# A two-layer decoder: filler products in waits of TensorE, and part of the next step's vector work between the two pieces of a double step

## The reference

```python
# layer 0
x = x + attention(ln(x))      # 1 head of 128, causal, softmax over the whole 512x512 matrix
x = x + cross(ln(x), ctx)     # 1 head, weights rounded to 256 levels, softmax over 77
x = x + experts(ln(x))        # 8 experts; each takes its own 128 tokens (top_k over tokens), GELU
# layer 1
x = x + attention(ln(x))      # 16 heads of 64, causal, softmax by row, output projection
x = x + cross_top(ln(x), ctx) # 16 heads of 8, the 32 largest of 77 scores per row, softmax, output projection
x = x + experts2(ln(x))       # 8 experts, each token takes its 2 best; relu(g) * u, then down
```

## Time and profile before

| | |
|---|---|
| median of 3 runs | 635.98 us (630.27 to 638.04) |
| the profiled execution | 634.84 us, span 633.10 us |
| PE busy | 545.8 us (86%) |
| PEld busy | 425.1 us (67%) |
| DVE busy | 409.1 us (65%) |
| ACT busy | 291.4 us (46%) |
| POOL busy | 208.6 us (33%) |
| mean granted clock | 0.937 |
| chain that ended last | PE 55%, DVE 20%, ACT 12%, issue 8%, POOL 5% |
| mean DMA rate | 30 GB/s |

### The profile page before, as it was taken

The page is one execution under the profiler, slowest core; times in us unless marked ns, Lnnn a source line. Parts: engine busy times, 40 slices in busy tenths (PEclk is TensorE's granted clock), DMA queues, the critical chain, the costliest instruction groups (busy, mean ns, idle before and its releaser), DMA issues.

```text
span 633.1 us, 11811 instructions
## 1 busy us (share of the span) xinstructions
PE 545.8 (86%) x3821; PEld 425.1 (67%) x3821; DVE 409.1 (65%) x2225; ACT 291.4 (46%) x721; POOL 208.6 (33%) x207
## 2 busy tenths in 40 slices
PE   4879768996789889899988688978977999899997
PEld 2565337874566656677667466658765878799997
DVE  3665654533443588886596698795895888844633
ACT  2332222333766565664764335562675555322221
POOL 4017200000434345653553335453363333250000
PEclk9996996997999999999999769896998999899999
DMA  4500101324000000000000000000440000010000
GB/s 136 166 1 15 50 13 51 104 63 150 2 1 1 1 1 3 0 2 2 1 2 1 2 0 2 2 2 1 158 139 0 19 14 19 18 35 1 26 1 9
DMA packets 23049, 19.16 MB, mean 30 GB/s; under 512 B 2048, under 2 KB 18508, under 8 KB 22989
## 3 DMA queue, kind: packets, MB, share of 16 engines
q1 hardware_dynamic: 22477, 17.36, 9.0%
q0 software_dynamic: 512, 1.05, 0.5%
HBM read 15.38 MB, written 3.01 MB: 29 GB/s over the span
## 4 chain that ended last, share of the span: by engine, by line
PE 55%; DVE 20%; ACT 12%; issue 8%; POOL 5%; DMA 0%; DVEq 0%; ACTq 0%; POOLq 0%
PE ps L1744 48%; DVE wk L1132 4%; ACT w_mem L1514 4%; DVE nmax L1068 3%; DVE top L1122 3%; ACT pr L1514 2%; ACT cat_mem L1498 2%; DVE sel_mem L961 2%; PE ps L2117 2%; PE ps L2179 1%; POOL xs_dram L737 1%; DVE xn L1095 1%; POOL wk L686 1%; POOL ex_mem L693 1%; PE ps L1756 1%
## 5 line engine op out<-in xcount | busy, mean ns | idle before, releaser
L1068 DVE TENSOR_REDUCE nmax<-ps 128x2 f32<-128x256 f32 (+1 forms) x64 | 51.2, 820 | 55.6 <-PE ps L1744 55.3
L1132 DVE MATCH_REPLACE8 wk<-top,wk 128x77 f32<-128x77 f32 x384 | 80.5, 223 | 0.0
L657 POOL TENSOR_TENSOR w_mem<-w_mem,rinv 128x256 f32<-128x256 f32 (+3 forms) x44 | 53.1, 1219 | 72.1 <-DVE rinv L1074 71.7
L1253 DVE TENSOR_TENSOR sel_mem<-gr,ps 128x512 f32<-128x512 f32 x47 | 32.2, 686 | 49.0 <-ACT gr L1687 48.2
L1744 PE MATMUL ps<-cat_mem 64*128 64x512 f32 (+7 forms) x272 | 54.4, 479 | 9.9 <-ACT cat_mem L1498 9.9
L1122 DVE MAX8 top<-wk 128x8 f32<-128x77 f32 x384 | 57.9, 223 | 0.0
L1687 ACT ACTIVATE gr<-ps 128x512 f32<-128x512 f32 x47 | 28.1, 598 | 63.1 <-PE ps L1744 63.1
L1514 ACT ACTIVATE w_mem<-ps,nmax 128x128 f32<-128x128 f32 (+3 forms) x88 | 44.5, 519 | 14.3 <-DVE nmax L1068 14.2
L595 POOL TENSOR_TENSOR rstd<-var_eps,minus_half 128x4 f32<-128x4 f32 x8 | 8.2, 1026 | 119.3 <-DVE var_eps L798 119.2
L686 POOL TENSOR_SCALAR wk<-wk 128x616 f32<-128x616 f32 x16 | 28.1, 1754 | 55.3 <-DVEq L1136 55.0
L657 POOL TENSOR_TENSOR pr<-pr,rinv 128x768 f32<-128x768 f32 (+3 forms) x20 | 26.7, 1343 | 34.9 <-DVE rinv L1074 34.8
(11 more groups left out here) (334 smaller groups left out, 1340.5 us busy)
## 6 DMA issues: line engine op xcount, KB each, us to landing
w_mem<-in_L_ffn_W_dram SPq DMA_DIRECT2D x12, 256.0 KB, 3.1
f_mem<-in_L_ffn_Wg_dram SPq DMA_DIRECT2D x8, 256.0 KB, 2.9
f_mem<-in_L_ffn_Wu_dram SPq DMA_DIRECT2D x8, 256.0 KB, 3.4
f_mem<-in_L_ffn_Wd_dram SPq DMA_DIRECT2D x8, 256.0 KB, 3.9
sel_mem<-in_L_ffn_W_dram SPq DMA_DIRECT2D x4, 256.0 KB, 4.9
xs_dram<-zero SPq DMA_DIRECT2D x1, 960.0 KB, 6.2
ys_dram<-f_mem SPq DMA_DIRECT2D x15, 64.0 KB, 1.5
xs<-xs_dram SPq DMA_DIRECT2D x3, 256.0 KB, 3.5
```

What stands on the lines that cost most here:

```text
L657: pool.tensor_tensor(pr[s][:, :, at:at + n], pr[s][:, :, at:at + n], rinv[:, i % 8, :].unsqueeze(2).to_broadcast([P, 2, n]), ALU.mult)\
L1068: dve.tensor_reduce(nmax[:, i % 8, :], ps[:, 2 * s:2 * s + 2, at:at + (c + 1) * P], X, ALU.max, negate=True).then_inc(nmax_ready, 1)
L1132: dve.match_replace(wk[q][:, t, h, :], top[q][:, t, h, 8 * r:8 * r + 8], src[:, t, h, :], GONE).then_inc(top_step, 1)
L1253: dve.tensor_tensor(hg[s][:, :], gr[s][:, :], ps[:, 2 * s + 1, :], ALU.mult)\
```

## The change

Five places get another order or one more instruction, and nine calls of `keep_busy` are added, which issue 65 filler products in all. Every output stays what it was.

- VectorE: `select(1, 1)` directly behind `select(0, 0)`.
- VectorE: `first_of(U)` holds what a step did first (`evac_cat`, `row_max(U+2)`, `row_inv(U+1)`); behind a double step U, `first_of(U+1)` is issued between pieces 2 and 3 of U.
- VectorE: `gate(13)` moves ahead of tile 12's piece.
- ScalarE: one GELU of a 128x1 column behind the exponential of the routing.
- TensorE: fillers in the last expert (6), before the rows of expert 0 are turned (4), before and behind the last scatter (4 and 4), before `norm_T(6)` (14), in `context_T` of steps 36 and 44 (4 each), in blocks 2 to 7 of the weight loading (3 each) and before `up_rows(0)` (7).

```diff
+def double_step(U):
+    n, r = piece_of(U) if 0 <= U < NU else (0, None)
+    return r == 2 and n >= 4
@@ VectorE, experts of layer 0
             select(0, 0)
+            select(1, 1)
             gate_of(0, 0)
             turn_sel(0, 0)
-            select(1, 1)
@@ VectorE, attention steps
-            for U in range(NU):
-                n, r = piece_of(U)
+            def first_of(U):
                 for j in range(4 * NP - 1):
                     if U == FIRST[j + 1] + 1:
                         evac_cat(j)
...
                     row_max(U + 2)
                 if U + 1 < NU:
                     row_inv(U + 1)
+            for U in range(NU):
+                n, r = piece_of(U)
+                if not double_step(U - 1):
+                    first_of(U)
...
                 if r is not None:
                     eight(n, r)
                     remove(n, r)
-                if r == 2 and n >= 4:
+                if double_step(U):
+                    first_of(U + 1)
                     eight(n, 3)
                     remove(n, 3)
@@ VectorE, experts of layer 1
             for j in range(NS):
-                gate(j)
+                if j != 13:
+                    gate(j)
...
                 if j == 12:
                     shares_of(1, 4, 2)
+                    gate(13)
                 cross(E + j)
@@ ScalarE
             act.activation(lg[:, :, :], lg[:, :, :], ACT.Exp)\
                .then_inc(elg_ready, 1)
+            act.activation(share0[:, 1:2], minus_half[:, 0:1], ACT.Gelu_apprx_tanh)
@@ TensorE, expert0
                 if e + 1 < E:
                     gather(e + 1, 1 - q)
                     spread(e + 1)
+                else:
+                    keep_busy(0, 6)
                 pe.wait_ge(h_ready, FC * (e + 1))
@@ TensorE, around the experts of layer 0
+            keep_busy(4, 4)
             turn_rows(0, 0)
...
                 expert0(e, e % 2)
+            keep_busy(0, 4)
             scatter(E - 1, 1)
+            keep_busy(0, 4)
@@ TensorE, context_T
+                if k < 2:
+                    keep_busy(7, 4)
                 pe.wait_ge(cn_ready, 2 * (k + 1))
@@ TensorE, start of layer 1
             pe.wait_ge(xin_ready, E)
+            keep_busy(4, 14)
             norm_T(6)
@@ TensorE, weight loading
+                if b >= 2:
+                    keep_busy(7, 3)
                 for k in range(2):
                     minus_hi(b, k)
...
             pe.wait_ge(w_lo_ready, 2 * E)
+            keep_busy(0, 7)
             up_rows(0)
```

More of the change, by code:

```diff
@@ L1160, in add_context @@
                 stats_two(k, gn_var)
-            row_max(0)
-            row_max(1)
-            row_inv(0)
-            for U in range(NU):
-                n, r = piece_of(U)
+            def first_of(U):
                 for j in range(4 * NP - 1):
@@ L1173, in _ @@
                     row_inv(U + 1)
+            row_max(0)
+            row_max(1)
+            row_inv(0)
+            for U in range(NU):
+                n, r = piece_of(U)
+                if not double_step(U - 1):
+                    first_of(U)
                 for k in range(3):
```

## The result

The changed kernel takes 644.56 us (median of 4 runs, 639.46 to 645.34) against 636.22 us (630.27 to 638.04) beside it: ratio 1.0113, 95% interval 1.0061 to 1.0165. The forecast was 626 us. The mean granted clock rose, from 0.937 to 0.950, and the kernel got slower all the same.

A forecast was written before the change was run, and what follows sets the result against it. TensorE was taken as the bound, over half the span, with twelve spells at 1.2 GHz. Terms -5.9 + 0.2 - 2.0 + 1.2 - 0.4 - 2.0 = -8.9 took 634.84 to 625.9, predicted 626 us; range 615 to 635.

The forecast's parts named there:

- The last expert, the scatter and the start of layer 1: Fillers there: +0.2 us for last expert, scatter and projections, -2.0 before norm_T(6) if the clock holds.
- the sum of the double steps: New order in steps 31, 34, 37, 40, 43, 46, with context_T fillers: +1.2 us, bounds -8 and +13.
- Step 31: Double step: fourth piece 1.3 us later, and TensorE waited for exactly the pick behind it: +1.3 us.
- Step 34: Double step: copy TensorE idled 3.52 us for comes 3.2 earlier, the pick is late next: -3.6 us.
- Steps 37 and 40: Double steps: TensorE's scores end after the third piece, VectorE stands before the fourth, partly taken up later: +2.0 us.
- Step 43: Double step: scores wait for a ScalarE copy, fourth piece slips 3.4 us, its turn had 0.21 spare: +3.4 us.
- Step 46: Double step: copy waits for half-clock products, slip paid back with more if the clock holds: -1.9 us.
- VectorE waits inside each pair: Rival, double steps: VectorE waits at the row maximum before the fourth piece: +13 instead of +1.2, 638 us; chance 0.10.
- The first rival: Double steps: the swap frees more, -6.8 us instead of +1.2, giving 618 us; chance 0.22.
- the third: Rival, all filler places: the clock does not hold and fillers cost time, together +7.5, or 642 us; chance 0.10.
- The port rival: GpSimd's mask holds VectorE's multiplications and last context's normalisation 2.6 us each: +5, 631 us; chance 0.06.
- gate(13): Layer 1's experts: gate moved ahead of the piece ends TensorE's 2.78 us wait, gate(14) late next: -2.0 us.

The follow-up runs named there:

- 3: The kernel before with the layer-0 edits alone: 628.57 us, ratio 0.9876.
- 5: Kernel 3 with the new order in all six double steps and ScalarE's copy of the cross scores no longer waiting for the fourth piece: 649.66 us, ratio 1.022.
- 9: Kernel 3 with the new order in steps 37 and 43 alone: 632.81 us, ratio 0.9966.
- 10: Kernel 3 with the new order in step 31 alone: 631.73 us, ratio 0.9956.
- 14: Kernel 3 with the new order in step 40 alone: 628.70 us, ratio 0.9870.
- 15: Kernel 3 with gate(13) ahead of tile 12's piece: 629.03 us, ratio 0.9795.
- 17: Kernel 12, but in step 34 only the copy between the pieces, row maximum and reciprocals back behind the fourth piece: 623.17 us, ratio 0.9796.
- 13: Kernel 3 with the new order in all six double steps and nothing else: 639.55 us, ratio 1.0106.
- 2: The kernel before with the new order of the double steps as its only edit: 653.04 us, ratio 1.017.
- 7: Kernel 3 with the new order in step 34 alone: 622.55 us, ratio 0.9665.
- 1: The changed kernel with the new order of the double steps undone, all else kept: 630.25 us, ratio 0.9874.
- 4: The changed kernel with the new order undone and gate(13) at its old place, layer 1's fillers kept: 629.14 us, ratio 0.9878.
- 12: Kernel 7 with step 37's addition of the context's projection put between the two pieces: 618.94 us, ratio 0.9741.
- 16: Kernel 12 with gate(13) forward and eight fillers in the wait for gate(14): 620.29 us, ratio 0.9810.

## Why the prediction was wrong

**What held.** The first experts: forecast -5.9, measured -6.1 (shift from +0.5 to -5.6), with the pitch and the whole clock that were named. The last expert, the scatter and the start of layer 1: forecast +0.2 - 2.0 = -1.8, measured -2.1. But that part does not hold in every execution: in seven of the seventeen traced kernels with these fillers (3, 5, 9, 10, 14, 15, 17) a spell of low clock that begins between 144 and 151 us takes 1.6 to 2.2 us of it back. The early GELU is within that. Weight loading: forecast -0.4; the shift goes from +7.97 to +7.82, -0.15. Kernel 3 shows layer 0's part by itself, -7.4 us in the median. (The 65 fillers come from eight added calls of `keep_busy`, not nine.)

**The step that failed** is the sum of the double steps, +1.2 in the forecast and +15.5 measured (+14.6 and +15.0 in kernels 13 and 2); the forecast's upper bound, +13, was too low. It failed in sign for step 46 and in size for steps 31, 37, 40 and 43:

- Step 31: forecast +1.3, the lengths of the moved instructions; measured +4.9. VectorE also waited for them (2.0 us), and the clock fell behind TensorE's two waits.
- Step 34: forecast -3.6, measured -4.7 in the changed kernel and -6.5 alone. The wait and the sign were right; the size beyond it is the clock's.
- Steps 37 and 40: forecast +2.0 together; measured +4.1 for 40 alone, and 37 is +3.0 in the changed kernel. I had counted the maxima's waits, not TensorE's wait for the addition behind the fourth piece, which grew from 0.5 us (layer 0's part) to 4.62 (kernel 9); with step 34 moved it was 2.47 already (kernel 7).
- Step 43: forecast +3.4; the fourth piece slipped by 3.2, and with what TensorE then waited for, 4.7 (37 and 43 alone: 7.3).
- Step 46: forecast -1.9, "paid back if the clock holds". Measured +4.3. The copy waited 3.85 us (437.94), and TensorE 3.56 us for the normalisation behind the fourth piece. The clock did not hold, and of the 4.3 us 3.4 are idle time.

Under all of them one thing was missing. I had followed from the fourth piece to the pick alone. Behind the same piece stand ScalarE's copy of the scores, the addition and the normalisation, each with TensorE waiting. The forecast put these waits at nothing. The runs show 12.7 us more idle time of TensorE in the stretch (kernel 13 against 3). The clock is not what was missing. Each of TensorE's waits of 2.4 to 4.6 us shown above in this stage does have a spell at 1.2 GHz behind or around it (from 325, 369, 396.5 and 441 us), but the kernel before has such spells too, and the mean clock of the stretch is 0.89 before and 0.90 after.

**The rivals.** "VectorE waits inside each pair" is what happened, with its place and the sign right. I gave it 0.10 and priced it at +13 for the stage. That the price comes so near is partly luck: it took +3.4 at each of five steps, while the fourth piece was to be held over 3 us in every pair; VectorE waited that long in step 46 alone. The argument against it, that the pieces and not TensorE are late, holds at step 34 alone. The first rival, that the swap frees more, is refuted by the sum. So is the third, that the clock does not hold, for the fillers of layer 0 (1.00 from 86 to 157 us). The port rival is refuted too: a normalisation beside the mask alone ran in 0.94 us, and beside a division with two inputs, and the pick behind it, in 3.43. VectorE first, then GpSimd:

```profile
376.19 3.43 DVE L1101 TENSOR_SCALAR xn<-x,mean_var,rstd 128x128 f32<-128x128 f32 x2
...
441.39 0.94 DVE L1101 TENSOR_SCALAR xn<-x,mean_var,rstd 128x128 f32<-128x128 f32 x2 [0.24 <-DVE wk L1138]
...
376.20 1.89 POOL L663 TENSOR_TENSOR w_mem<-w_mem,rinv 128x1024 f32<-128x1024 f32 x1
...
441.30 1.75 POOL L692 TENSOR_SCALAR wk<-wk 128x616 f32<-128x616 f32 x1 [7.37 <-DVEq L1142]
```

I had weighed a rule of the Trainium skill ("SBUF — State Buffer", "SBUF: two separate sides"): a VectorE operation with two SBUF inputs and a GpSimd operation that reads SBUF exclude each other for a whole instruction; so do a VectorE operation in a mode that takes both ports and one of GpSimd. These rows show what the earlier trace rows showed: the operation that gets longer has two-input operations of GpSimd beside it, and the one-input mask did not hold it. The normalisation has one tensor as input, though, and no row shows in which mode it ran; the multiplications of the earlier trace rows remain the test of the rule.

**gate(13)**: forecast -2.0, measured +1.5. The schedule was right (gate(14) is late next, and the shift fell by 1.9 us, to +6.0 at 553.19; the wait that went was 2.78 us, not the 3.8 of the expectations). The clock that fell behind the new wait brought the shift to +9.3. That fall was the term put at nothing.

## What to carry to other kernels

Before work is moved into a gap between two pieces of an engine's queue, ask when its input is ready: a moved instruction that must wait is a delay for all that stands behind it, and it should be moved only where somebody waits for its result and its input is already there (here one of six steps). List everything behind the delayed instruction, on every engine, not only the chain that is late today; freeing the one that shows uncovers the next. Measure a new wait with the clock behind it: behind gate(14) it turned -1.9 us into +1.5, while over the double steps the mean clock did not change and the waits were nearly the whole price (12.7 of 14.6 us).

## What the runs showed that was not expected

Code that is the same does not meet the clock in the same place: the 7.1 us by which kernels with the same instructions differ at 300 us are as much as layer 0's part gains. The Trainium skill ("TensorE: Matmul & The Clock Gate", "Part 1: The HAM clock gate") says that the chip's judging of TensorE's activity runs free of the kernel, so that the same kernel meets it in another phase from run to run; the traces agree as far as they go. For measuring it means that a difference of 3 us between medians of six runs says little here. The same stretch of two traces says more, and TensorE's idle time in it more still: in three pairs of kernels with the same code there (3 and 15, 1 and 4, 12 and 16) the stretch differs by 1.5, 2.7 and 3.5 us, the idle time by 0.1 at most.
